# Quaternion memory: all products of key with value and memory made by VectorE; the expert stage's second product lags three units

## The reference, cut to what matters

```python
x = x + time_mixing(layernorm(x))          # L0 attention
x = x + top1_experts(layernorm(x))         # L0 feed-forward
x = x + memory(layernorm(x))               # L1 attention, the stage changed here
x = x + top4_experts(layernorm(x))         # L1 feed-forward, changed here too
# memory:
keys = (x @ Wk.T + bk).reshape(B, L, 32, 4); keys = keys / norm(keys)
values = (x @ Wv.T + bv).reshape(B, L, 32, 4)
memory = jnp.cumsum(quat_mul(values, keys), axis=1)
retrieved = quat_mul(memory, quat_conj(keys)).reshape(B, L, D)
retrieved = retrieved / jnp.sqrt(positions); normed = layernorm(retrieved)
x + (normed @ Wo.T + bo)
# top4_experts: 32 experts of width 64 and one shared expert of width 128, D = 128
y_e = (silu(x @ W1[e]) * (x @ W3[e]) * weight[e]) @ W2[e]
```

## Time and profile before

| | before |
|---|---|
| median of 3 runs | 898.77 us (896.37 to 899.38) |
| the profiled execution | 899.56 us, its span 897.7 us |
| busy share: PE, DVE, ACT, POOL | 85%, 71%, 52%, 54% |
| granted TensorE clock, mean | 0.913 of full speed |
| memory stage, one tile in its steady part | 14.93 us |
| top-4 experts, one tile in its steady part | 42.1 us |

### The profile page before, as it was taken

One profiled execution on the slowest core, in us unless ns is written; L12 is line 12 of the kernel. 1 busy time (PEld: TensorE's weight loads), 2 busy tenths in 40 slices (PEclk: granted clock), 3 DMA queues, 4 the chain that ended last, 5 costly groups with the idle time before them and its releaser, 6 DMA issues.

```text
span 897.7 us, 14530 instructions
## 1 busy us (share of the span) xinstructions
PE 765.0 (85%) x3937; PEld 567.5 (63%) x3938; DVE 633.8 (71%) x1453; ACT 464.0 (52%) x918; POOL 485.7 (54%) x440
## 2 busy tenths in 40 slices
PE   5999999996486499912889998999999999999997
PEld 2444444542386499912778786677768686868685
DVE  3789999986564255574587876768686868786764
ACT  3455555652121377722464645656656565756453
POOL 2677777773046344561355653555555555555554
PEclk9999999997555699965899999899999999999998
DMA  5000000000491122220000003545547281909180
GB/s 178 0 1 1 1 0 0 0 1 0 93 375 47 42 66 68 62 106 1 1 2 1 1 1 81 112 91 112 115 88 142 61 168 36 191 20 195 38 166 12
DMA packets 35663, 60.08 MB, mean 67 GB/s; under 512 B 3488, under 2 KB 15264, under 8 KB 34960
## 3 DMA queue, kind: packets, MB, share of 16 engines
q1 hardware_dynamic: 33328, 54.67, 26.1%
q0 software_dynamic: 2272, 4.67, 1.5%
HBM read 51.04 MB, written 8.28 MB: 66 GB/s over the span
## 4 chain that ended last, share of the span: by engine, by line
PE 26%; issue 12%; POOL 11%; DVE 3%; ACT 2%; POOLq 0%; ACTq 0%; DVEq 0%
POOL d_hid_lo L2000 6%; PE c_m L1507 2%; PE c_m L1509 2%; PE c_m L1508 2%; PE c_o L1558 1%; PE c_r L1558 1%; PE c_k L1507 1%; POOL c_bound L1967 1%; PE c_r L1488 1%; PE c_k L1508 1%; PE c_k L1509 1%; POOL c_read L1973 1%; PE c_o L1556 1%; PE c_o L1555 1%; PE c_v L1509 1%
## 5 line engine op out<-in xcount | busy, mean ns | idle before, releaser
L2000 POOL TENSOR_TENSOR d_hid_lo<-c_bound,d_hid_hi 128x512 fp32r<-128x512 f32 x136 | 176.4, 1297 | 157.5 <-ACT d_hid_hi L1930 155.5
L1930 ACT ACTIVATE d_hid_hi<-c_bound 128x512 fp32r<-128x512 f32 x136 | 85.2, 626 | 45.3 <-DVE c_bound L1798 44.9
L576 POOL TENSOR_TENSOR a_rs<-a_r,a_state 128x512 f32<-128x512 f32 x64 | 75.2, 1186 | 29.9 <-DVE a_state L419 28.0
L419 DVE TENSOR_TENSOR_SCAN a_state<-a_decay,a_state,a_vb 128x512 f32<-128x512 f32 x64 | 81.1, 1269 | 0.0
L1092 POOL DMA_INDIRECT results<-b_y_row,b_result_row x39 | 37.4, 960 | 51.1 <-DVE b_y_row L1008 29.8
L1789 DVE TENSOR_TENSOR c_m<-c_bound,c_m 128x512 f32<-128x512 f32 x64 | 44.2, 691 | 26.8 <-PE c_m L1509 20.9
L1789 DVE TENSOR_TENSOR c_v<-c_bound,c_v 128x512 f32<-128x512 f32 x64 | 44.2, 691 | 24.3 <-PE c_v L1509 19.0
L1507 PE MATMUL c_m<-d_x_hi,d_hi 128*128 128x512 f32 x136 | 56.1, 413 | 1.8 <-DVE c_bound L1798 1.6
L999 DVE TENSOR_TENSOR b_hidden<-b_h,b_b 128x512 f32<-128x512 f32 x39 | 27.0, 691 | 42.9 <-PE b_h L835 42.2
L1509 PE MATMUL c_m<-d_x_hi,d_lo 128*128 128x512 f32 x136 | 54.1, 398 | 0.0
L1508 PE MATMUL c_m<-d_x_lo,d_hi 128*128 128x512 f32 x136 | 54.0, 397 | 0.0
(11 more groups left out here) (306 smaller groups left out, 2178.4 us busy)
## 6 DMA issues: line engine op xcount, KB each, us to landing
d_w_wide<-pair_weights SPq DMA_DIRECT2D x64, 512.0 KB, 11.8
b_w<-in_w SPq DMA_DIRECT2D x2, 2048.0 KB
d_raw<-in_moe SPq DMA_DIRECT2D x3, 1088.0 KB
b_xin<-rows_in SPq DMA_DIRECT2D x39, 64.5 KB
b_rows<-results SPq DMA_DIRECT2D x4, 512.0 KB, 5.0
out<-c_read SPq DMA_DIRECT2D x8, 256.0 KB, 2.5
a_weights<-in_mixing SPq DMA_DIRECT2D x1, 901.0 KB
shape_consts<-in_consts SPq DMA_DIRECT2D x1, 744.0 KB
```

The lines of the kernel that those rows point to most:

```text
L419: dve.tensor_tensor_scan(state[:, j, seq_cols(h, 1)], decay[:, h, :], vb[j % 3][:, :], first, ALU.mult, ALU.add).then_inc(scan_ready, 1)
L576: pool.tensor_tensor(rs[:, j, :], rr[:, h, :], state[:, j, seq_cols(h, 0)], ALU.mult).then_inc(rs_ready, 1)
L1930: act.activation(hid_hi[:, r, :], hidden[:, r, :], ACT.Copy).then_inc(hi_ready, 1)
L2000: pool.tensor_tensor(hid_lo[:, r, :], hidden[:, r, :], hid_hi[:, r, :].bitcast(F32), ALU.subtract).then_inc(lo_ready, 1)
```

## The change

Three things change. First, in the memory stage DVE makes all four groups of both products, in one loop each, and POOL none; the normalised value stays in PSUM for all four groups, the normalised memory in SBUF. Second, in the expert stage the second product of a unit is issued three units later instead of two (`LAG`), with three buffers (`HALVES`) for its two halves instead of two, and the pieces of `end` come one unit later. Third, the identity matrix gets a buffer and a load of its own, so that the large table of constants can be given up after the first stage.

```diff
+LAG = 3
+HALVES = 3
...
-        hid_hi = dsb("hid_hi", [P, 2, TILE], F32R)
-        hid_lo = dsb("hid_lo", [P, 2, TILE], F32R)
+        hid_hi = dsb("hid_hi", [P, HALVES, TILE], F32R)
+        hid_lo = dsb("hid_lo", [P, HALVES, TILE], F32R)
...
                     if step == 4:
-                        need(pe, bound_dve, 2 * i)
+                        need(pe, bound_ready, SUB * i)
                         project(bank_v, "bv", "wv", xt).then_inc(v_out, 1)
...
-                    if u >= 2:
-                        second(i, h, u - 2)
+                    if u >= LAG:
+                        second(i, h, u - LAG)
...
-                    if u == 4:
+                    if u == 5:
                         pe.wait_ge(y_ready, i + 1)
...
                 def main(i, h, step):
                     if step == 0:
-                        dve.wait_ge(valuen_ready, 2 * (i + 1))
+                        dve.wait_ge(valuen_ready, i + 1)
                         dve.wait_ge(key_ready, i + 1)
                         need(dve, memory_out, SUB * i)
-                        for s in (0, 1):
+                        for s in range(SUB):
                             dve.tensor_tensor(in_quats(bound[:, s, :, :]), in_quats(key[:, h, s, :, :]),
-                                              spread_component(early_value[:, s, :]), ALU.mult).then_inc(bound_dve, 1)
+                                              spread_component(value[:, s, :]), ALU.mult).then_inc(bound_ready, 1)
...
                     if step == 10:
                         dve.wait_ge(memoryn_ready, 2 * (i + 1))
                         need(dve, read_out, i)
-                        for s in (0, 1):
+                        for s in range(SUB):
                             dve.tensor_tensor(in_quats(read[:, s, :, :]), in_quats(key[:, h, s, :, :]),
-                                              spread_component(early_n[:, s, :]), ALU.mult).then_inc(read_dve, 1)
+                                              spread_component(memory_n[:, s, :]), ALU.mult).then_inc(read_ready, 1)
...
                 def end(i, h, u):
-                    if u == 5:
+                    if u == 6:
                         dve.wait_ge(yt_out, i + 1)
...
                 def split(n, r):
                     act.wait_ge(hidden_ready, n + 1)
-                    need(act, unit_out, n - 1)
-                    act.activation(hid_hi[:, r, :], hidden[:, r, :], ACT.Copy).then_inc(hi_ready, 1)
+                    need(act, unit_out, n + 1 - HALVES)
+                    act.activation(hid_hi[:, n % HALVES, :], hidden[:, r, :], ACT.Copy).then_inc(hi_ready, 1)
...
-                    if u == 3:
+                    if u == 4:
                         act.wait_ge(unit_out, UNITS * (i + 1))
...
-                    if step == 0:
-                        pool.wait_ge(valuen_ready, 2 * i + 1)
-                        pool.wait_ge(key_ready, i + 1)
-                        need(pool, memory_out, SUB * i)
-                        for s in (2, 3):
-                            pool.tensor_tensor(in_quats(bound[:, s, :, :]), in_quats(key[:, h, s, :, :]),
-                                               spread_component(value_n[:, s - 2, :]), ALU.mult).then_inc(bound_pool, 1)
...
-            time_mixing(nc, x_tok, consts, x_in.rearrange(by_group, p=P), a_in, c_in, [(router, b_in)])
+            time_mixing(nc, x_tok, consts, x_in.rearrange(by_group, p=P), a_in, c_in,
+                        [(router, b_in), (ident, c_in[:, 0:P])])
```

More of the change, by code:

```diff
@@ L1574, in unit @@
                     three(bank_3[r][:, :], hi[1][:, cols], lo[1][:, cols], x_hi[:, h, :], x_lo[:, h, :]).then_inc(h3_out, 1)
-                    if u >= 2:
-                        second(i, h, u - 2)
-                    elif not (isinstance(i, int) and i == 0):
-                        second(i - 1, 1 - h, UNITS - 2 + u)
+                    if u >= LAG:
+                        second(i, h, u - LAG)
+                    elif i > 0:
+                        second(i - 1, 1 - h, UNITS - LAG + u)
                 def end(i, h, u):
-                    if isinstance(i, int) and i == TILES - 1 and u < 2:
-                        second(i, h, UNITS - 2 + u)
-                    if u == 4:
+                    if i == TILES - 1 and u < LAG:
+                        second(i, h, UNITS - LAG + u)
+                    if u == 5:
                         pe.wait_ge(y_ready, i + 1)
@@ L1656, in main @@
                         need(dve, read_out, i)
[L1657 removed]
+                        for s in range(SUB):
                             dve.tensor_tensor(in_quats(read[:, s, :, :]), in_quats(key[:, h, s, :, :]),
[L1659 removed]
+                                              spread_component(memory_n[:, s, :]), ALU.mult).then_inc(read_ready, 1)
                     if step == 12:
                         need(dve, got_ready, i)
[L1662 to L1665 removed]
+                        k0 = key[:, h, :, 0, 0:P:QC]
+                        dve.tensor_tensor(components(real[:, :, :]), components(memory_n[:, :, :]),
+                                          k0.unsqueeze(3).broadcast_to([P, SUB, QUATS, QC]), ALU.mult).then_inc(real_ready, 1)
                 def tail(i, h, step):
                     if step == 0:
[L1669 removed]
+                        dve.wait_ge(real_ready, i + 1)
                         dve.wait_ge(read_out, i + 1)
@@ L1998, in unit @@
                     pool.wait_ge(hi_ready, n + 1)
-                    need(pool, unit_out, n - 1)
-                    pool.tensor_tensor(hid_lo[:, r, :], hidden[:, r, :], hid_hi[:, r, :].bitcast(F32), ALU.subtract).then_inc(lo_ready, 1)
+                    need(pool, unit_out, n + 1 - HALVES)
+                    pool.tensor_tensor(hid_lo[:, n % HALVES, :], hidden[:, r, :], hid_hi[:, n % HALVES, :].bitcast(F32),
+                                       ALU.subtract).then_inc(lo_ready, 1)
                 def end(i, h, u):
```

72 lines of the change are left out of this document (22 added, 50 removed).

## The result

The changed kernel takes 912.48 us (median of 4 runs, 911.36 to 913.72), the kernel before in the same session 899.08 us. The ratio is 1.0153 [1.0124, 1.0182]: 13 us slower. I had forecast +2.8 us, so 901.6, with a range up to 905.5; the result lies outside it. The profiled execution has a span of 909.5 us at a mean granted clock of 0.904, against 897.7 us and 0.913.

The account below looks back on a forecast made before the run. It took a closed loop of engine waits, 14.93 us per memory tile, and PE's waits on DVE and POOL in 42.1 us expert tiles as the bounds. Memory +7.7 and experts -4.9 gave +2.8, so 901.6 us, range 896 to 905.5.

Parts of the forecast that it names:

- the clock's term: Memory stage: PE's busy share falls from 14.93 to 16.12 us bodies, but no clock fall expected; costed at nothing.
- Rival 3: PE's clock falls or the pipeline restarts badly: a second half-speed stretch adds 3 us, collisions as much; 905 to 908; chance 0.12.
- 1.19 us per body in the ring: Memory stage's closed loop of engine waits: two more DVE products after `c_got` add 1.19 us; 7.1 us in bodies 1 to 6.
- `c_shift` stays held by `c_kept`: Memory stage: POOL still issues `c_kept` right behind `c_rstd`, so DVE's `c_shift` keeps its 1.22 us.
- The reads are hidden: Memory stage: two added `c_read` products on DVE fit ahead of its idle 1.87 us before `c_got`, costing nothing.
- Body 7, +1.6: Last memory body: products add 1.19 us, routing behind four reads 1.2, a shorter `d_weight` gives back 0.8; +1.6 us.
- Front of body 0, -1.0: Before the first memory body: without POOL's `c_bound` the shift is short, 0.15 for 1.11 us, so projection starts 1.0 us earlier.
- Experts, -4.9: Expert stage: lag three removes `d_hid_lo` waits, a held `d_shift` takes 0.6 back in tiles 1 to 5; -4.9 us in all.
- the transfer wait: Start of the experts: PE idles 0.7 us longer there; half-speed stretch of about 6 us taken as unchanged, bound 3 us.
- Rivals 1, 2 and 4: `d_shift` not held, 898.1 us (0.18); all `d_hid_lo` waits vanish, 890 (0.1); memory stage has hidden slack, 893 (0.05).

Follow-up runs that it names:

- e3_fill: Changed kernel plus five unused PE matmuls in bodies 1 to 6, ahead of PE's wait for the last `c_memory`; 902.13 us, ratio 1.0033.
- e11_idle_only: Kernel before, POOL keeping its products, with DVE making its own two `c_bound` again into an unread buffer, and PE waiting for them; 918.65 us, ratio 1.0227.
- e7: Kernel before with lag three, three buffers, later `end` and all four `c_read` on DVE, POOL still making its `c_bound`; 906.66 us, ratio 1.0141.
- e2: Kernel before with only the lag of three, three buffers, later `end` pieces and the identity's own buffer; 896.19 us, ratio 0.9968.
- e8: Kernel before with lag three, `end` pieces in their old units and POOL's `c_kept` in step 0; 884.04 us, ratio 0.9883.
- e6: Kernel before with lag three and three buffers, but the `end` pieces in their old units; 887.18 us, ratio 0.9922.
- e4: Changed kernel with POOL's `c_kept` moved from step 4 to step 0, ahead of `c_rstd`; 895.23 us, ratio 0.9958.
- e9: Kernel before with lag three and all `c_read` on DVE, POOL's `c_bound` waiting for DVE's reads of the tile before; 893.99 us, ratio 0.9942.
- e1: Changed kernel with lag two, two buffers and old `end` units put back, leaving the memory-stage change; 917.57 us, ratio 1.0197.
- e5: Changed kernel plus two unused PE matmuls in bodies 1 to 6, ahead of PE's wait for the last `c_memory`; 904.77 us, ratio 1.0110.
- e10: Changed kernel with POOL's `c_kept` in step 0 and the `end` pieces in their old units; 892.75 us, ratio 0.9939.

## Why the prediction was wrong

The step that failed is the last sentence of the costs, where the clock's term was put at nothing: "In the memory stage PE's busy share falls in the ratio of 14.93 to 16.12; in body 7 it is already as low, 13.25 of 16.0, at a clock of 1.00, so I expect no fall." In the traced execution the clock fell in every body but the first, which cost 10.9 us in bodies 2 to 6 and some 0.5 in body 7. e3_fill shows that PE's wait is what brings it (fill it, and 10.9 us come back with all else in place), e11_idle_only that the wait is enough. The argument took a busy share over a whole body for the measure. The rows speak against that measure: e7's bodies are idler than the changed kernel's (PE busy 14.14 of 16.80 us, against 14.18 of 16.10), and the first four of its intervals are at 1.00; of the first six only the fifth has a fall. Its windows:

```profile
458.00:474.80 16.80, 13.81 (x105) 12.19 (x105) 13.79 (x34) 8.52 (x23) 6.34 (x7) 1.00 0.00 1
474.80:491.60 16.80, 14.14 (x108) 12.47 (x108) 14.20 (x34) 8.53 (x23) 6.34 (x7) 1.00 0.00 1
```

and PE's waits:

```profile
484.04 0.50 PE L1448 MATMUL c_o<-c_bias,c_ones 64*128 64x512 f32 x1 [0.87 <-ACT c_normed_t L1875]
...
487.28 0.91 PE L1486 MATMUL c_r<-c_read,ident 128*128 128x128 f32 x6 [1.66 <-DVE c_read L1652]
```

What differs is where the idle lies. Three waits of together 1.92 or 2.14 us lie within 3.3 us in the changed kernel and in e11; in e7 there are 2.5 us, but 0.87 ahead of `c_o` and 1.66 ahead of `c_r`, with `c_o`'s matmuls between them; in body 7 of the earlier trace rows the idle is spread as well. This reading of e7 is argued from its trace; no run here moved the same idle from one place to another. It isn't the whole of it either: body 7 has spread idles in the kernel before, e2, e8 and e6 alike, and e6's fell. The runs show that the added wait brings the falls, and leave open by what measure. In the changed kernel none of PE's three idles ahead of the fall at 468.4 is above 1 us (0.99, 0.28 and 0.87). Rival 3 had the fall of the clock, with a chance of 0.12 and at the wrong place and size: one stretch more of 3 us, where six of the seven bodies have one.

Point by point:
- *1.19 us per body in the ring*: right. The first body is 16.12; without the clock (e3) the six intervals cost 6.8, forecast 7.1. One of them, 15.27 before, gave 0.3 back.
- *`c_shift` stays held by `c_kept`*: right, 1.22. e4 shows what that was worth: 1.05 us a body.
- *The reads are hidden*: right in the steady bodies (e9); that e7 alone missed shows how much it hung on what POOL does in that time.
- *Body 7, +1.6*: the routing's `d_weight` is short, 0.28, as forecast, and the interval is 1.94 longer, with a half-speed stretch in it. e1 and e5 have the same body 7 at a clock of 1.00, and both take 17.90, which is 1.48 more than before. So the forecast 1.6 was right without the clock, and the stretch cost the other 0.46. The windows of e1 and of the changed kernel:

```profile
552.20:570.10 17.90, 14.04 (x121) 12.40 (x119) 15.46 (x54) 8.68 (x22) 3.62 (x5) 1.00 0.02 5
549.41:567.77 18.36, 15.17 (x121) 13.73 (x119) 15.47 (x53) 8.68 (x22) 3.62 (x5) 0.91 0.02 5
```

- *Front of body 0, -1.0*: wrong in its mechanism. The shift is still 1.07, since `c_kept` takes `c_bound`'s place. The way to the first `c_got` is 1.1 shorter all the same, but that the number fits is luck: over the kernels of this case this way takes from 33.7 to 36.1 us, and the granted clock comes back from 0.50 to stay at 1.00 on it at different times, 22.4 us behind the stage's start in the changed kernel and 24.6 in the one before.
- *Experts, -4.9*: measured -4.6. `d_shift` is held, 0.96; steady tiles 41.70; waits for `hidden` in place of those for `d_hid_lo`; the transfer wait grew from 4.10 to 4.37 and its half-speed stretch is as long as before, some 6.8 us. Rivals 1, 2 and 4 are out: `d_shift` takes 0.96, tiles 41.7 and not 40, bodies longer.

## What to carry to other kernels

Where the matrix engine sits in a ring with other engines, price a wait that is added beside a wait it already has twice: once as delay (here 6.8 us in six turns), and once as a possible fall of the clock (here 10.9 us more in the same six). Look at the idles in front of `PE` rows one by one, and not only at the busy share of a whole turn, which misled here. That closeness matters is the likely reading, not a tested one; the cheap test is a filler like e3's. And when work leaves an engine whose instructions held another's in the trace (here POOL's, with 1.22 us for `c_shift` and 1.38 for `c_memory_n`), ask which of its instructions now comes earlier, and what it will hold there.

## What was not expected of the hardware

- Turns of 16.12 us with idles of 0.77 or 0.99, then 0.28 and 0.87 us close together lost the full clock in 14 of 18 turns (bodies 1 to 6 of the changed kernel, e1 and e11). With two idles of at most 0.28 and 0.87 they kept it in 16 of 16 (e3, and bodies 1 to 5 of e4 and e10). In between, at 1.4 to 1.7 us in all, 5 of 8 lost it (e5, and body 6 of e4 and e10), with equal idles in turns that fell and turns that didn't.
- A fall costs a turn in bodies 1 to 6 either some 1.6 or some 3.0 us (1.5 to 1.65 or 2.8 to 3.15 over all kernels), and nothing between. In body 7 one cost 0.5 (changed kernel against e1) and one 0.8 (e6 against e2).
- One idle of 3.27 us at the start of the experts left the clock at 1.00 in e3, where three of under 1 us each had cost it in the changed kernel's loop.
- More work on PE made the kernel faster: five useless matmuls in a 0.99 us wait took 1.2% off the changed kernel.
